# An attention and expert block on one core: a new order of work on every engine, residual gates multiplied into weights, a router in fewer steps

## What is computed

```python
mod = silu(c) @ wmod                       # per batch: sa, ca, ga, sb, cb, gb, each 512 wide
ga, gb = sign * maximum(abs(.), 0.25)      # the two residual gates
h = layernorm(x) * (1 + ca) + sa
q, k, v = rope(h @ Wq), rope(h @ Wk), h @ Wv           # 16 heads of 32
out = g0 * attention(compressed keys, 64 blocks of 16 tokens) \
    + g1 * attention(16 selected tokens) \
    + g2 * attention(window of 128 tokens)              # g = softmax(h @ Wg + bg)
x = x + ga * (out @ Wo + bo)
h = layernorm(x) * (1 + cb) + sb
s = weights of the best 2 of 6 experts, from softmax(h @ router_W + router_b), normalised
x = x + gb * (h @ base_W.T + base_b + shared low-rank term + sum over e of s[e] * routed low-rank term e)
```

## Time and profile before

| | us |
|---|---|
| runs | 3261.16, 3259.92, 3257.35 (median 3259.92) |
| profiled execution, its own time | 3262.03 |
| its span (first to last instruction) | 3260.2 |
| TensorE busy | 2517.7 (77%) |
| DVE busy | 1918.1 (59%) |
| ScalarE busy | 1451.9 (45%) |
| GpSimd busy | 796.1 (24%) |

### The profile page before, as it was taken

One profiled execution on the slowest core, in us unless ns is written; L12 is line 12 of the kernel. 1 busy time (PEld: TensorE's weight loads), 2 busy tenths in 40 slices (PEclk: granted clock), 3 DMA queues, 4 the chain that ended last, 5 costly groups with the idle time before them and its releaser, 6 DMA issues.

```text
span 3260.2 us, 55786 instructions
## 1 busy us (share of the span) xinstructions
PE 2517.7 (77%) x18184; PEld 1573.5 (48%) x18184; DVE 1918.1 (59%) x4932; ACT 1451.9 (45%) x4829; POOL 796.1 (24%) x708
## 2 busy tenths in 40 slices
PE   5878778678876778877777787777887777886776
PEld 2645555345544555445554455544555455553443
DVE  3545665466654667456664556645666456764665
ACT  1344444354443555344553444534444345543453
POOL 1422232222211322122321222312222222221121
PEclk8978888689897889878888888887888778987887
DMA  5100000100001000000000000000000100000000
GB/s 171 36 4 20 21 17 11 30 14 21 21 7 34 17 14 24 25 13 17 20 17 27 11 20 17 17 27 11 21 21 14 27 17 14 21 17 23 14 17 14
DMA packets 40661, 73.85 MB, mean 23 GB/s; under 512 B 6529, under 2 KB 6529, under 8 KB 40354
## 3 DMA queue, kind: packets, MB, share of 16 engines
q1 hardware_dynamic: 31138, 53.21, 5.3%
q10 hardware_dynamic: 9216, 16.78, 1.4%
HBM read 53.15 MB, written 16.83 MB: 21 GB/s over the span
## 4 chain that ended last, share of the span: by engine, by line
issue 68%; POOL 19%; PE 6%; DVE 3%; ACT 1%; DMA 1%; POOLq 0%; SPq 0%; DVEq 0%; ACTq 0%
POOL csp L1170 5%; POOL css L1162 4%; POOL ra L1154 2%; POOL xc L1183 2%; POOL ra L1188 2%; POOL vec L1150 1%; POOL vea L1146 1%; PE ps_m L484 1%; POOL h_lo L1176 1%; POOL kr L1154 1%; ACT pw L945 1%; PE ps_m L486 1%; PE ps_m L485 1%; DVE ps_s L1387 1%; DMA wb_s<-wb_in 1%
## 5 line engine op out<-in xcount | busy, mean ns | idle before, releaser
L945 ACT ACTIVATE pw<-ps_s,wmax 128x128 f32<-128x128 f32 x1024 | 360.0, 377 | 168.4 <-DVE wmax L1392 168.4
L1413 DVE COPY_PREDICATED pT<-keep_prev,ps_t 128x512 f32<-128x512 uint32 x224 | 163.7, 731 | 453.1 <-PE ps_t L584 443.0
L484 PE MATMUL ps_m<-w_hi,h_hi 128*128 128x512 f32 x768 | 360.7, 470 | 69.5 <-ACT zT L971 31.3
L955 ACT ACTIVATE pw<-pw,wden 128x128 f32<-128x128 f32 x1024 | 313.5, 392 | 91.9 <-DVE wden L1402 86.7
L601 PE MATMUL ps_s<-cst,csp 128*128 128x128 f32 x960 | 192.6, 334 | 177.9 <-POOL csp L1170 143.0
L978 ACT ACTIVATE pT<-ps_s 128x512 f32<-128x512 f32 x240 | 142.1, 592 | 402.0 <-PE ps_s L601 401.7
L485 PE MATMUL ps_m<-w_lo,h_hi 128*128 128x512 f32 x768 | 313.8, 409 | 0.0
L486 PE MATMUL ps_m<-w_hi,h_lo 128*128 128x512 f32 x768 | 313.4, 408 | 0.0
L671 PE MATMUL ps_m<-wbt_s,h2T 128*128 128x512 f32 x512 | 276.3, 631 | 1.5 <-DVE gl L1375 1.5
L1424 DVE TENSOR_REDUCE cm<-css 128x16 f32<-128x256 f32 (+1 forms) x128 | 98.9, 815 | 266.4 <-ACT css L925 266.4
L638 PE MATMUL ps_m<-wo_s,aT 128*128 128x512 f32 x512 | 246.3, 609 | 0.8 <-ACT aT L982 0.8
(11 more groups left out here) (191 smaller groups left out, 4989.2 us busy)
## 6 DMA issues: line engine op xcount, KB each, us to landing
xa<-x_in SPq DMA_DIRECT2D x65, 256.0 KB, 2.7
xc<-x_in SPq DMA_DIRECT2D x64, 256.0 KB, 2.6
out<-t ACTq DMA_DIRECT2D x64, 256.0 KB, 2.0
gbc<-gate_rows SPq DMA_DIRECT2D x24, 256.0 KB, 5.0
pw<-wmod_in SPq DMA_DIRECT2D x3, 1024.0 KB, 5.4
pT<-wmod_in SPq DMA_DIRECT2D x3, 1024.0 KB, 5.2
qT<-wqkv_in SPq DMA_DIRECT2D x2, 1024.0 KB, 8.7
v_s<-wqkv_in SPq DMA_DIRECT2D x1, 1024.0 KB, 11.9
```

Source lines behind the costliest of these rows:

```text
L484: pe_.matmul(ps[:], h_hi[:, c, :], w_hi[:, col, c, :], start=(c == 0), stop=False)
L945: ins = act.activation(pw[:, hw, :], ps_w[:, j, i, 1, :], ACT.Exp, bias=wmax[:, hw:hw + 1], accum_out=wden[:, 0, hw:hw + 1])
L955: act.activation(pw[:, hw, :], pw[:, hw, :], ACT.Copy, scale=wden[:, 2, hw:hw + 1]).then_inc(wn_ok, 1)
```

## The change

1. All three lists of calls are rewritten on every engine, and with them the bank orders. In a slot, K now shares bank 1 with Q and is taken in four pieces between other units; QT, G, H2T and Z follow each other in bank 0.
2. `ga` and `gb` are no longer applied by DVE. SyncE reloads `wo_s`, `wbt_s` and `wb_s` from HBM for each of the seven further batches, and POOL multiplies them by the gate rows: `scale_out` (four instructions of 128x512) at the end of `turn`, `scale_feed` (five) in `first_slot`. `residual` and `final` become one addition each, out of PSUM.
3. The router takes 13 steps in place of 16: the softmax is not normalised before the best two are taken, and the `1e-6` is scaled by the sum instead.
4. `compress` is cut into four pieces of two tiles, spread over the turn; the waits for h_hi and for `rotate` move into `split_h` and `rope`.

The core of the diff (both other lists of TensorE, those of ScalarE, and the router's lines are left out):

```diff
-R_STEPS = 16
+R_STEPS = 13
...
-SLOT_ORDER = [("HT", 1), ("Y", 0), ("Q", 1), ("K", 0), ("H2T", 1), ("QT", 0), ("Z", 1), ("G", 0), ("KT", 1), ("F", 0),
-              ("ZT", 1), ("V", 1)]
...
+SLOT_ORDER = [("Y", 0), ("HT", 1), ("Q", 1), ("K", 1), ("QT", 0), ("G", 0),
+              ("H2T", 0), ("Z", 0), ("KT", 1), ("F", 0), ("ZT", 1), ("V", 1)]
...
             def load_gates(b):
-                sp.wait_ge(o_ok, NT * b + 1)
+                sp.wait_ge(xb_ok, NT * b + 1)
...
                     load_xa(NT * (b + 1) + NT - 2, (b + 2) % B, 0)
+                    load_gates(b + 1)
+                    sp.wait_ge(*m_full_at("loop", b, "Y", NT - 1))
+                    load_out()
+                    sp.wait_ge(*m_full_at("loop", b, "F", NT - 1))
+                    load_feed()
...
+            def compress(seg, b, ba, tiles):
...
             def slot(seg, b, s):
...
+                output(seg, b, t, [0])
                 if a:
                     transpose_h(seg, b, t, Ta)
-                output(seg, b, t, [0, 1])
                 window_scores(b, s, 0)
-                output(seg, b, t, [2, 3])
-                if a:
-                    project(seg, b, t, "Q", 0)
+                output(seg, b, t, [1, 2, 3])
+                if a:
+                    project(seg, b, t, "Q", 0, [0, 1, 2, 3])
                 window_scores(b, s, 1)
                 if a:
-                    project(seg, b, t, "K", 1)
+                    project(seg, b, t, "K", 1, [0])
                 transpose_window(b, s, 0)
+                if a:
+                    project(seg, b, t, "K", 1, [1])
+                    transpose_rot(seg, b, t, Ta, "QT", ra, 1)
+                    gate_logits(seg, b, t, [0, 1])
+                    project(seg, b, t, "K", 1, [2])
+                    gate_logits(seg, b, t, [2, 3])
+                    project(seg, b, t, "K", 1, [3])
                 transpose_h2(seg, b, t)
-                if a:
-                    transpose_rot(seg, b, t, Ta, "QT", ra, 1)
+                window_values(b, s, 0)
+                transpose_window(b, s, 1)
                 transpose_cs(b, s, 0)
                 lora_down(seg, b, t)
-                window_values(b, s, 0)
-                transpose_window(b, s, 1)
...
+            def scale_out(b):
+
+                gp.wait_ge(d_wo, 16 * (b + 1))
+                gp.wait_ge(d_gbc, 16 * (3 * b + 3))
+                for c in range(NC):
+                    gp.tensor_tensor(wo_s[:, c, :], wo_s[:, c, :], gbc[:, 0, :], ALU.mult).then_inc(wo_ok, 1)
+
+            def scale_feed(b):
+
+                gp.wait_ge(d_wf, 32 * (b + 1))
+                for c in range(NC):
+                    gp.tensor_tensor(wbt_s[:, c, :], wbt_s[:, c, :], gbc[:, 1, :], ALU.mult).then_inc(wf_ok, 1)
+                gp.tensor_tensor(wb_s[:, :], wb_s[:, :], gbc[0:NZ + 1, 1, :], ALU.mult).then_inc(wf_ok, 1)
...
             def slot(seg, b, s):
...
+                residual_in(b, t)
                 if a:
                     split_h(Ta)
-                residual_in(b, t)
+                deviation_c(NT * b + t)
                 cs_subtract(b, s)
-                deviation_c(NT * b + t)
                 if a:
                     rotate(seg, b, t, Ta, "Q", ra)
+                cs_normalise(b, s)
+                if a:
                     rotate(seg, b, t, Ta, "K", kr)
-                cs_normalise(b, s)
-                if a:
+                    deviation_a(Ta + 1)
                     weigh_keys(seg, b, t, Ta)
-                    deviation_a(Ta + 1)
...
-                dve.wait_ge(o_ok, T + 1)
-                dve.wait_ge(d_out, 16 * (T + 1))
-                dve.tensor_tensor(t1[:], ps[:], gbc[:, 0, :], ALU.mult).then_inc(done, 1)
+                if t:
+                    dve.wait_ge(*m_done_at(seg, b, "F", t - 1))
+                dve.wait_ge(xb_ok, T + 2)
+                dve.tensor_tensor(x1[:], ps[:], xc[:, t % 2, :], ALU.add).then_inc(done, 1)
                 dve.wait_ge(*m_done_at(seg, b, "Y", t))
-                dve.wait_ge(xb_ok, T + 2)
-                dve.tensor_tensor(x1[:], t1[:], xc[:, t % 2, :], ALU.add).then_inc(y_ok, 1)
-                dve.wait_ge(y_ok, T + 2)
                 ln_stats(x1[:], stc, mvc, vec, lnc, T)
...
-                dve.tensor_tensor(t1[:], ps[:], gbc[:, 1, :], ALU.mult).then_inc(done, 1)
-                dve.wait_ge(*m_done_at(seg, b, "F", t))
-                dve.tensor_tensor(t1[:], x1[:], t1[:], ALU.add).then_inc(o_ok, 1)
+                dve.wait_ge(d_out, 16 * (T + 1))
+                dve.tensor_tensor(t1[:], ps[:], x1[:], ALU.add).then_inc(done, 1)
...
                 window_weights(b, s, 0)
                 if a:
                     rope(seg, b, t, "Q")
-                ln_scale(x1[:], mvc, vec, xc[:, t % 2, :], lnc, lncp, NT * b + t)
                 window_max(b, s, 1)
                 cs_factor(b, s)
-                if a:
-                    dve.wait_ge(rope_ok, 2 * Ta + 2)
+                ln_scale(x1[:], mvc, vec, xc[:, t % 2, :], lnc, lncp, NT * b + t)
+                if a:
+                    gates_soft(seg, b, t, Ta, 0)
+                split_probs(b, s, 0)
+                if a:
                     rope(seg, b, t, "K")
-                split_probs(b, s, 0)
+                    sum_q(seg, b, t, Ta)
+                router(seg, b, t, 0)
+                split_probs(b, s, 1)
                 window_weights(b, s, 1)
-                split_probs(b, s, 1)
-                router(seg, b, t, 0)
-                if a:
-                    gates_soft(seg, b, t, Ta, 0)
-                    sum_q(seg, b, t, Ta)
+                router(seg, b, t, 1)
+                if a:
+                    ln_a(seg, b, s - 1, Ta + 1, s)
+                final(seg, b, t)
                 split_probs(b, s, 2)
-                router(seg, b, t, 1)
                 split_probs(b, s, 3)
```

More of the change, by code:

```diff
@@ L505, in gate_logits @@
                     mm.then_inc(full, 1)
-            def compress(ba):
-                pe_.wait_ge(cv_done, ba + 1)
-                pe_.wait_ge(s_done, QUADS * ba + quad(0, 1) + 2)
+            def compress(seg, b, ba, tiles):
                 dst = ps_cv[NB:P, :]
-                pe_.matmul(dst, pew[:, :], pe_s[:, :], start=True, stop=False, skip_group_check=True)
-                for t in range(NT):
+                if tiles[0] == 0:
+                    pe_.wait_ge(cv_done, ba + 1)
+                    pe_.wait_ge(s_done, QUADS * ba + quad(0, 1) + 2)
+                    pe_.matmul(dst, pew[:, :], pe_s[:, :], start=True, stop=False, skip_group_check=True)
+                for t in tiles:
+                    if t == NT - 1:
+                        pe_.wait_ge(*m_done_at(seg, b, "V", t))
                     off = NB - 8 - 8 * t
@@ L1461, in router @@
                 base = R_STEPS * T
-                n = [0 if part == 0 else 2]
-                def step(ins):
-                    n[0] += 1
-                    ins.then_inc(r_ok, 1)
-                    if n[0] != 2:
-                        dve.wait_ge(r_ok, base + n[0] + 1)
+                logit, negmax, total, e = ro[:, 0:E], ro[:, 6:7], ro[:, 7:8], ro[:, 8:8 + E]
+                order, chosen, index = ro[:, 24:32], ro[:, 32:32 + E], ro[:, 40:42]
+                norm = ro[:, 42:43]
                 if part == 0:
@@ L1497, in router @@
-                assert n[0] == R_STEPS
+                dve.max_index(roi[:], order, ro[:, 8:16]).then_inc(r_ok, 1)
+                dve.tensor_scalar(norm, total, 1e-6, ro[:, 24:25], ALU.mult, ALU.add).then_inc(r_ok, 1)
+                dve.wait_ge(r_ok, base + 5)
+                dve.tensor_copy(index, roi[:, 0:2]).then_inc(r_ok, 1)
+                dve.wait_ge(r_ok, base + 6)
+                dve.tensor_tensor(norm, norm, ro[:, 25:26], ALU.add).then_inc(r_ok, 1)
+                dve.wait_ge(r_ok, base + 7)
@@ new lines, in router @@
+                dve.tensor_scalar(chosen, cst[:, C_IO:C_IO + E], ro[:, 40:41], None, ALU.is_equal).then_inc(r_ok, 1)
+                dve.wait_ge(r_ok, base + 8)
+                dve.reciprocal(norm, norm).then_inc(r_ok, 1)
+                dve.wait_ge(r_ok, base + 9)
+                dve.scalar_tensor_tensor(out=chosen, in0=cst[:, C_IO:C_IO + E], scalar=ro[:, 41:42], in1=chosen,
+                                         op0=ALU.is_equal, op1=ALU.add).then_inc(r_ok, 1)
+                dve.tensor_copy(zr[:, 0:R], zs[:, 0:R]).then_inc(r_ok, 1)
@@ new lines, in router @@
+                dve.wait_ge(r_ok, base + 11)
+                dve.scalar_tensor_tensor(out=chosen, in0=chosen, scalar=norm, in1=e, op0=ALU.mult, op1=ALU.mult
+                                         ).then_inc(r_ok, 1)
+                dve.wait_ge(r_ok, base + 13)
+                dve.tensor_tensor(zr[:, R:NZ].rearrange("p (e r) -> p e r", e=E),
+                                  zs[:, R:NZ].rearrange("p (e r) -> p e r", e=E),
+                                  chosen.unsqueeze(2).broadcast_to([P, E, R]), ALU.mult).then_inc(r_ok, 1)
```

326 lines of the change are left out of this document (167 added, 159 removed).

## The result

The changed kernel takes 2561.8 us (median of four runs, 2561.1 to 2566.6). Before, the four runs beside it have a median of 3260.5. The ratio is 0.786, with a 95% interval of 0.784 to 0.788: 699 us less.

What follows compares the result with a forecast made beforehand. TensorE with its waits, chiefly for K's bank, was taken to bound the kernel. A pass of 60 + 6 x 38 + 42 = 330 replaces 399.4 us, 486 less in seven: 2776 from 3262.0, median 2774, range 2650 to 2930.

Steps and rivals of the forecast that it cites:

- What bounds the kernel: In a slot, TensorE's 5.39 us wait at Q's transposition is for K's bank, held until DVE's late rope of K.
- Rival 5: In the slot, QT really waits for DVE, so the slot stays near 45.3 less 3: 3130 us, chance 0.03.
- I take about half, 38 us: New slot: between 36.3 us at full clock and 39.3 with the old clock loss, 38 taken.
- The waits in the new slot: TensorE's waits in a hand layout of the new slot: 3.3 us in place of 9.1.
- A slot of TensorE's work ... 33 us: A slot without waits and at full clock: 45.0 - 9.1 - 3 = 32.9, say 33 us.
- Router and residual: DVE in a slot: residual from 2.5 to 0.7 us, router three steps fewer at some 0.2 each, 0.6.
- First slot: First slot of a pass: 57.3 us in the layout, made 60, 13.6 less than 73.6.
- Epilogue and prologue: Outside the loop's passes: a change of 0 taken, within 15 us either way.
- Rival 1: Whole pass as laid out with the clock full, 84.8 us less per pass: 2666 us, chance 0.13.
- Rival 2: In the slot, POOL's subtraction locks out DVE's small multiplication, 2.5 us per slot: 2880 us, chance 0.17.
- Rival 3: At the loop's edge, POOL's nine multiplications are on the path, 80 us: 2855 us, chance 0.05.
- Rival 4: In the slot, new waits replace the old, TensorE at 1.2 GHz for much of it: 49.5 us, 3436, chance 0.04.

Runs made afterwards that it cites:

- order and router: The changed kernel with the residual gates applied by DVE again and the router of 13 steps kept: 2688.9 us.
- the ladder: Four kernels, each the changed one with one wait added on TensorE ahead of K's first chunk, 1.4 to 3.2 us in the trace: 2585.2 to 2764.7 us.

## Why the prediction was too high

The forecast for the profiled execution was 2776, and it is 2562.3: 214 too high. Step by step:

- **What bounds the kernel** was right. QT waited for K's bank (rope of K moved ahead halves that wait), and the order is most of the gain. Rival 5 is out.
- **"I take about half, 38 us"**, the surcharge of 1.7 us for a fallen clock, is the step that failed by most: 42 x 1.7 = 71 us. The six slots show 1.00, so the term measured nothing. I reasoned from many waits close together. That is not absurd, as order and router shows with 1.0 us a slot, but the kernel has fewer and shorter ones than I laid out, and a row of mine said that 0.35 and 0.75 were followed by fast work. (I gave the five pieces as 2.4 us; my list makes them 2.6.) Without this term the forecast is 2705, still 143 too high: the steps below err in the same direction, all but the last.
- **The waits in the new slot**, 3.3 us, are 1.9 to 2.0: some 57 us. At K 0.75 (laid out 0.7 to 1.2), at the gate logits 0.69 (0.8), at the first values 0.46 (0.5). The other five, at the second scores, QT, H2T, the router and the third split, 1.3 in all, are absent. The layout by hand finds the places and sizes of the waits on the main chain, and adds small ones that don't come.
- **"A slot of TensorE's work ... 33 us"** is 32.4: 25 us.
- **Router and residual**: "some 0.2 each, 0.6" is 1.45 us for the router. Its consequence was seen (it "lets DVE keep up"), and sized by nothing; measured, gates and router are worth 187 us in the new order. This is no term of the sum below, since the layout had the saving in it.
- **First slot** 60 forecast, 53.2 measured, 7 x 6.8 = 48. The "issue" at the loop's edge was to stay at 6.7 and is 3.6; the h_lo wait is 3.45 (3), the 4.21 is 1.45 (1.5), the 4.08 is 2.96 (3.5). The loop's edge alone is 3.1 of the 6.8 us. **Turn** 42 forecast, 41.0 measured, 7.
- **Epilogue and prologue** at 0 are 24 us less, outside my 15.
- In the other direction, the pass that I cut before, 399.4 us, was longer than the mean of seven, 396.7: 19 us.

71 + 57 + 25 + 48 + 7 + 24 - 19 = 213. The range failed with them: its lower end stood 16 us below the layout taken at its word (2666), so an error of the layout itself, which came to some 100 us, had no room in it.

- **Rival 1**, no surcharge, 2666, was right on the clock of the slots and got 0.13; it is still 104 too high, by the waits, the first slot and the ends.
- **Rival 2**: its mechanism is there, its price is not. In the slot VectorE's small multiplication starts at 1519.18, inside POOL's subtraction, and ends at 1519.55; the subtraction is two instructions, the first ends at 1519.53, and so the lockout lasts some 0.14 us. Had it come 0.4 us later, it could have met the second, of 1.9 us, as one of the 128 did (1.87 us). That it comes where it does is luck, and no step of the forecast. The rows are in the last section.
- **Rival 3** is out by the run without the multiplications. **Rival 4** named the true danger with a price that the ladder bears out in kind: with 3.2 us in one piece, the slot grows by 4.5 us, of which 2.5 are the clock. It would need far more to lose 9 us a slot.
- The new addition at 0.68 was right: all 64 of L1514 take 0.67 to 0.69 us. The Trainium skill, page "SBUF — State Buffer", section "Who interferes with whom", says that a DVE instruction with at most one SBUF input, outside the two-port modes, does not contend with GpSimd. The trace agrees: only 8 of the 64 have POOL at work beside them, but L1563, of the same form, has it 49 times and takes 0.68 to 0.69. Before, L1455 with both inputs in SBUF took 2.31 us (median) in the 48 cases beside POOL and 0.69 in the 16 without.

## What to carry to other kernels

Lay out a new order by hand with the durations of the old trace, and trust the places of the waits on the main chain; but give the layout itself an error, since here it was some 100 us too long in all. Price the clock as a range: in these kernels a single wait of 2 us or more was followed by falls in many slots, one of 0.75 or 1.4 us never, and several of 0.5 to 0.7 close together in one kernel and not in another. In a schedule where TensorE waits 2 us in 34, the engines that it takes results from are critical: gates and router, worth 102 us together in the old order, are worth 187 in the new one. And a wait that is filled on TensorE alone may come back longer behind the next result, as it did with the gate logits.
